# Four edits to a two-layer gated cross-attention kernel: output banks of the last FFN, lead-in of the second attention, start of the quantised down product, slot order of the first attention

## The reference, cut to what matters

```python
x = x + tanh(g_xattn[0]) * attention0(layernorm(x), ctx)   # 16 heads of 16, biases on q, k, v, out
x = x + tanh(g_ffn[0])   * ffn0(layernorm(x))              # 256 -> 768 gate and up, 4-bit block-quantised
                                                           # weights, activations rounded to 16-bit codes
x = x + tanh(g_xattn[1]) * attention1(layernorm(x), ctx)   # 8 heads of 64
x = x + tanh(g_ffn[1])   * ffn1(layernorm(x))              # 256 -> 1024, butterfly, exact gelu, butterfly,
                                                           # 1024 -> 256
# ffn0: every act_qdq needs the largest |value| of its whole tensor before one code can be made
#   o = act_qdq(act_qdq(gate * sig) * up);  return o @ lpbq_dequant(w_down).T
# ffn1, seen as the kernel computes it: the two butterflies are linear, so they are folded into the weights
#   y = gelu(x @ W1 + b1) @ W2 + b2
```

## Time and profile before

| what | value |
|---|---|
| median of 3 runs | 1124.44 us |
| profiled execution: its own time | 1123.65 us |
| its span | 1121.8 us |
| TensorE busy | 971.8 us (87%) |
| VectorE busy | 789.1 us (70%) |
| ScalarE busy | 620.1 us (55%) |
| mean granted TensorE clock | 0.934 |

### The profile page before, as it was taken

One profiled execution on the slowest core, in us unless ns is written; L12 is line 12 of the kernel. 1 busy time (PEld: TensorE's weight loads), 2 busy tenths in 40 slices (PEclk: granted clock), 3 DMA queues, 4 the chain that ended last, 5 costly groups with the idle time before them and its releaser, 6 DMA issues. The chain is left out here.

```text
span 1121.8 us, 20570 instructions
## 1 busy us (share of the span) xinstructions
PE 971.8 (87%) x6833; PEld 862.0 (77%) x6833; DVE 789.1 (70%) x1588; ACT 620.1 (55%) x1088; POOL 231.4 (21%) x424
## 2 busy tenths in 40 slices
PE   6489999998399997546699976999999989999998
PEld 5367788876378876445689965999999977888888
DVE  5358888865369888879678725677777858556662
ACT  4157766665367699779477435555656533222230
POOL 4223333311186000000022202111112113111210
PEclk9789999999689998867899986999999989999999
DMA  6745555560233077598333455755555410001001
GB/s 193 222 122 142 141 145 148 148 218 10 107 130 150 29 236 243 194 334 308 121 108 115 162 192 131 166 121 123 123 123 123 98 39 1 19 20 38 19 20 38
DMA packets 102807, 143.60 MB, mean 128 GB/s; under 512 B 42950, under 2 KB 76742, under 8 KB 100438
## 3 DMA queue, kind: packets, MB, share of 16 engines
q1 hardware_dynamic: 102438, 141.67, 43.7%
q0 software_dynamic: 304, 1.10, 0.3%
HBM read 76.30 MB, written 47.13 MB: 110 GB/s over the span
## 5 line engine op out<-in xcount | busy, mean ns | idle before, releaser
L41 PE MATMUL bank<-f_xt_hi,f_w_hi 128*128 128x512 f32 x320 | 130.1, 406 | 11.9 <-DMA f_xt_lo<-x_spill 8.7
L42 PE MATMUL bank<-f_xt_lo,f_w_hi 128*128 128x512 f32 x320 | 127.3, 398 | 0.0
L43 PE MATMUL bank<-f_xt_hi,f_w_lo 128*128 128x512 f32 x320 | 127.0, 397 | 0.0
L2635 ACT ACTIVATE f_h<-bank,f_b 128x512 f32<-128x512 f32 x64 | 43.4, 691 | 122.3 <-PE bank L43 74.5
L599 ACT ACTIVATE a_prob<-bank 77x512 f32<-77x512 f32 x128 | 72.7, 593 | 21.1 <-PE bank L763 20.9
L41 PEld LDWEIGHTS bank<-f_xt_hi,f_w_hi 128*128 128x128 f32 x320 | 61.8, 193 | 27.9 <-DMA f_xt_lo<-x_spill 10.8
L665 DVE TENSOR_REDUCE a_maxima<-bank 128x4 f32<-128x308 f32 x128 | 60.7, 474 | 31.8 <-PE bank L738 30.1
L41 PE MATMUL bank<-f_w_hi,f_h_hi 128*128 128x256 f32 x256 | 72.6, 284 | 8.1 <-DVE xres L2600 8.1
L43 PE MATMUL bank<-f_w_hi,f_h_lo 128*128 128x256 f32 x256 | 72.2, 282 | 0.0
L42 PE MATMUL bank<-f_w_lo,f_h_hi 128*128 128x256 f32 x256 | 72.2, 282 | 0.0
L43 PEld LDWEIGHTS bank<-f_xt_hi,f_w_lo 128*128 128x128 f32 x320 | 61.7, 193 | 13.4
(11 more groups left out here) (317 smaller groups left out, 3066.3 us busy)
## 6 DMA issues: line engine op xcount, KB each, us to landing
u_spill<-f_ubuf SPq DMA_DIRECT2D x48, 256.0 KB, 2.5
f_uback<-u_spill SPq DMA_DIRECT2D x24, 512.0 KB, 5.8
a_stack<-a_queries SPq DMA_DIRECT2D x16, 512.0 KB, 4.8
a_q_max<-a_q_hi SPq DMA_DIRECT2D x32, 256.0 KB, 4.8
a_kb<-a_key_spill SPq DMA_DIRECT2D x96, 77.0 KB, 2.5
f_mats<-in_low_steps SPq DMA_DIRECT2D x12, 512.0 KB, 6.8
xres<-in_x SPq DMA_DIRECT2D x16, 256.0 KB, 4.4
a_queries<-a_q_hi SPq DMA_DIRECT2D x16, 256.0 KB, 3.0
```

Source lines behind the costliest of these rows:

```text
L41: nc.tensor.matmul(out, w_hi, m_hi, start=start, stop=False)
L42: nc.tensor.matmul(out, w_hi, m_lo, start=False, stop=False)
L43: return nc.tensor.matmul(out, w_lo, m_hi, start=False, stop=stop)
L2635: act.activation(h[:, n % 2, :], hbank[n % 4][:, :], ACT.Gelu, bias=b1[:, n:n + 1]).then_inc(h_ready, 1)
```

## The change

1. Last FFN: four banks for the four y tiles, the two new ones being banks three and four of the h products. The waits follow: y tile n of a group waits for tile n of the group before; y tiles 2 and 3 also wait until the GELU has read the seventh and eighth h product of the next group out of those banks; the third and fourth h product wait for the adds of y tiles 2 and 3.
2. Quantised FFN, last block: `hi` moves up among the weight units on ScalarE, and `prod` on TensorE; the rounding of the first queries goes ahead of the last three value moves; both halves of the values are fetched after the last save instead of the first half after the sixth save.
3. Second attention: for the first batch ScalarE issues the four query transfers, and the two small ones for the gate and bias; SyncE's step is skipped; the second `pick` rounding goes behind the first queries' roundings; GpSimd clears `q_max` before `kz`.
4. First attention: other orders in PE_SLOT, ACT_SLOT and DVE_SLOT (the strings for the lead-in slots stay).

```diff
-        DVE_SLOT = "w0 mx0 norm mx1 ln mx2 w1 w2 w3 mx3 xs mx4 am w4 mx5 as mx6 w5 mx7 qs pu st1".split()
+        DVE_SLOT = "mx0 xs mx1 norm mx2 w0 w1 w2 mx3 ln mx4 w3 mx5 as mx6 am w4 mx7 qs pu st1 w5".split()
...
                 if what == "qm":
                     if isinstance(b, int) and b == 0:
-                        sp.wait_ge(mt_cleared, HPC)
+                        return
...
-                    if isinstance(b, int) and b == 0:
-                        sp.dma_start(gate_raw[:], gate).then_inc(small_in, 16)
-                        sp.dma_start(bo_raw[:], gbias).then_inc(small_in, 16)
...
-            pool.memset(kz[1][:].bitcast(F32), 0.0).then_inc(kb_cleared, 1)
             for a in range(HPC):
                 pool.memset(q_max[a][:].bitcast(F32), 0.0).then_inc(mt_cleared, 1)
+            pool.memset(kz[1][:].bitcast(F32), 0.0).then_inc(kb_cleared, 1)
...
+                    if isinstance(b, int) and b == 0 and n == 1:
+                        pick(1)
+                        act.wait_ge(q_rounded, NP)
+                        for q in (q_both, q_max):
+                            if q is q_max:
+                                act.wait_ge(mt_cleared, HPC)
+                            for a in range(HPC):
+                                act.dma_start(q[a][own[a], par, :, :].bitcast(F32),
+                                              q_hi[own[a], :, :].bitcast(F32)).then_inc(hi_in[par], 16)
...
-                    if i == NV // 2:
-                        fetch_values(0, i)
+                fetch_values(0, NV)
                 fetch_values(1, NV)
...
-                for n in range(4):
+                weights(0)
+                hi(0)
+                weights(1)
+                weights(2)
+                hi(1)
+                weights(3)
+                weights(4)
+                hi(2)
+                for n in range(5, 9):
                     weights(n)
-                hi(0)
-                weights(4)
-                hi(1)
-                weights(5)
-                weights(6)
-                hi(2)
-                weights(7)
-                weights(8)
                 hi(3)
...
-                for n in range(5):
+                for n in range(3):
                     weights(n)
                 prod(0)
-                for n in range(5, 7):
+                for n in range(3, 5):
                     weights(n)
                 prod(1)
-                for n in range(7, 9):
+                for n in range(5, 9):
                     weights(n)
...
-        ybank = [O0, O1]
+        ybank = [O0, O1, hbank[2], hbank[3]]
...
-                    if not (isinstance(g, int) and g == 0 and n < 2):
-                        pe.wait_ge(y_added, g * GTT + n - 1)
+                    if n >= 2:
+                        last_h = min(g + 2, G) if isinstance(g, int) else g + 2
+                        pe.wait_ge(h_ready, last_h * HT + n - 3)
+                    if n < 2 and not (isinstance(g, int) and g == 0) or isinstance(g, int) and g == G - 1:
+
+                        pe.wait_ge(y_added, g * GTT + n + 1 - GTT)
```

More of the change, by code:

```diff
@@ L406, in stacked_attention @@
         Q_MOVES, K_MOVES = 2, 6
-        PE_SLOT = "s0 s1 t3 mx0 s2 s3 mx1 xt p1 s4 mx2 s5 at0 mx3 p3 s6 mx4 s7 p5 mx5 q0 t0 mx6 t1 q1 mx7 pr0 pr1 mt t2 p7".split()
-        ACT_SLOT = "s0 s1 s2 s3 st2 s4 p1 xt s5 at0 p3 s6 xn q1 p5 s7 mt p7".split()
-        DVE_SLOT = "w0 mx0 norm mx1 ln mx2 w1 w2 w3 mx3 xs mx4 am w4 mx5 as mx6 w5 mx7 qs pu st1".split()
+        PE_SLOT = "s0 s1 xt mx0 s2 t3 s3 mx1 s4 q0 mx2 p1 s5 mx3 p3 s6 mx4 s7 at0 mx5 t0 q1 mx6 p5 t1 mx7 pr0 pr1 mt t2 p7".split()
+        ACT_SLOT = "s0 s1 xt s2 st2 s3 p1 s4 s5 p3 s6 at0 q1 s7 xn p5 mt p7".split()
+        DVE_SLOT = "mx0 xs mx1 norm mx2 w0 w1 w2 mx3 ln mx4 w3 mx5 as mx6 am w4 mx7 qs pu st1 w5".split()
         POOL_SLOT = "ln xn st1".split()
@@ L1060, in _, with pick @@
         def _(act):
+            def pick(n):
+                act.activation(kb[:, n, :, 1, :, :], late["pick_raw"][:, :, :, 0:S], ACT.Copy).then_inc(picked, 1)
             def step(what, b, par):
@@ L1063, in step @@
                     if isinstance(b, int) and b == 0:
+                        act.dma_start(gate_raw[:], gate).then_inc(small_in, 16)
+                        act.dma_start(bo_raw[:], gbias).then_inc(small_in, 16)
                         act.wait_ge(late["pick_in"], 16)
-                        for n in range(2):
-                            act.activation(kb[:, n, :, 1, :, :], late["pick_raw"][:, :, :, 0:S], ACT.Copy).then_inc(picked, 1)
+                        pick(0)
                         return
@@ L2301, in _ @@
                             round_key(n)
+                    if b == 16:
+                        act.wait_ge(first.xt_ready, 1)
+                        act.activation(xt_hi, T1[:, :].rearrange("p (c t) -> p c t", c=DC), ACT.Copy).then_inc(first.xt_rounded, 1)
                     for i in range(NV):
@@ L2322, in _ @@
                         last.then_inc(first.ln_xn, 1)
-                    if b == 16:
-                        act.wait_ge(first.xt_ready, 1)
-                        act.activation(xt_hi, T1[:, :].rearrange("p (c t) -> p c t", c=DC), ACT.Copy).then_inc(first.xt_rounded, 1)
                     i, half = (b - 4) // 3, (b - 4) % 3
@@ L2599, in step @@
                     x = xtile(g, n)
-                    dve.scalar_tensor_tensor(out=x, in0=ybank[n % 2][:, 0:D], scalar=tg[:, 0:1], in1=x,
+                    dve.scalar_tensor_tensor(out=x, in0=ybank[n][:, 0:D], scalar=tg[:, 0:1], in1=x,
                                              op0=ALU.mult, op1=ALU.add).then_inc(y_added, 1)
@@ L2655, in step @@
                         pe.wait_ge(xt_split, (g + 1) * DC)
-                    if not (isinstance(g, int) and g == 0 and n < 4):
+                    if n in (2, 3) and not (isinstance(g, int) and g < 2):
+                        pe.wait_ge(y_added, g * GTT + n - 3 - GTT)
+                    elif not (isinstance(g, int) and g == 0 and n < 4):
                         pe.wait_ge(h_ready, g * HT + n - 3)
@@ L2665, in step @@
                         pe.wait_ge(h_split, (g + 1) * HT)
-                    if not (isinstance(g, int) and g == 0 and n < 2):
-                        pe.wait_ge(y_added, g * GTT + n - 1)
+                    if n >= 2:
[3 more added lines that the diff above has]
+                        pe.wait_ge(y_added, g * GTT + n + 1 - GTT)
                     for m in range(HT):
-                        last = three_passes(nc, ybank[n % 2][:, 0:D], h_hi[:, par, m, n * P:(n + 1) * P],
+                        last = three_passes(nc, ybank[n][:, 0:D], h_hi[:, par, m, n * P:(n + 1) * P],
                                             h_lo[:, par, m, n * P:(n + 1) * P], w2_hi[:, m, :], w2_lo[:, m, :],
```

## The result

The kernel before took 1124.51 us in the median of 4 runs (1119.17 to 1129.31), the changed kernel 1110.58 us in 4 (1108.23 to 1113.65). The ratio is 0.9874, 95% interval 0.9828 to 0.992. Later, beside 11 runs of before, six more runs of the changed kernel gave 0.9898 (0.9851 to 0.9944). The profiled execution took 1113.65 us, with a span of 1111.9; that of before had a span of 1121.8. It is 9.9 us shorter.

The account below looks back on a forecast made before the run. The prediction took TensorE, busy 87% of the span, to set the pace, with time lost at its stops. Its terms, 9.6 + 0.8 + 6.8 - 1.0 = 16.2 us off 1123.65, gave 1107.5 us; range 1101 to 1113.5.

Parts of the forecast that it names:

- Last FFN: Last FFN: with four banks TensorE no longer stops six times for VectorE's adds; 9.6 us gained, low end 8.1.
- The lead-in: Second attention, opening to first scores: queries come earlier, but both value halves precede the keys; 1.0 us lost, bounds +1.6 and -4.6.
- the second rival: Second attention's lead-in: values, keys and queries share the DMA engines, first scores at +17.6 instead of +14.0; 1111 us, chance 0.14.
- the prediction's own sign: Forecast is wrong if the last FFN's groups keep 25 us, or the seam's stop only moves into the next block.
- what-is-late-next: Last FFN: GELUs end 1.5 us before y tiles 2 and 3 need them; adds have over 4 us of margin.
- the third rival: Last FFN: adds of y tiles 2 and 3 or the GELUs hold up TensorE for half the gain; 1112 us, chance 0.06.
- Down product's start: Quantised FFN's down product: starts 3.3 us earlier, but two units now follow; 0.8 us gained, bounds -2.8 and +3.3.
- Seam: Quantised FFN to second attention: first query matmuls start 5.5 us sooner and at full clock; 7.8 us gained.
- Slot orders: First attention: a 0.29 us hole goes every second slot, small waits are added; net 0.1 a slot, 1.0 us lost.
- the keys' loop: First attention: 7.2 us from last scores to `mx0`, while query and key transfers are issued and land; expected to stay.
- The first rival: First attention: the slot orders pay and slots take 13.17 us; 1102 us in all, chance 0.14.
- the fourth: First attention: ScalarE paces the slots, each losing about 1.5 us, 13 times; 1126 us, slower than before, chance 0.05.

Follow-up runs that it names:

- the banks and codes alone: Kernel before with only the last FFN's four banks and the codes' rounding moved up among the weight units; 1117.06 us, ratio 0.9918.
- the run with the slot orders alone: Kernel before with only the three new slot orders of the first attention; 1126.29 us, ratio 1.0009.
- the pair of the seam alone: Kernel before plus early rounding of x and both value fetches after the last save; with ScalarE's transfers 1127.06 us, with SyncE issuing 1125.53.
- the pair with the second half late: Changed kernel with the values' second half fetched behind the second batch's keys: 1105.73 and, again, 1104.6 us; with SyncE issuing queries, gate and bias 1109.35.
- the seam and lead-in kernel: Kernel before plus early rounding of x, both value fetches after the last save, and ScalarE issuing gate, bias and queries; 1127.06 us, ratio 0.9987.

## Why the prediction was right, and which term was not

It forecast 16.2 us off; the medians show 13.9 (1124.51 - 1110.58), the second measurement 10.5 (1124.24 - 1113.78). The terms as measured below give 9.4 + 2.1 + 1.5 - 0.8 = 12.2. The profiled pair differs by less, 9.9: the changed one had its long last slot (5.3 us against it), while the one before took 2.4 us more from its first scores to the last FFN.

The direction was earned, by the last FFN above all. That the time fell so near was in part luck. The lead-in was wrong by 5.4 us; the down product gave 1.3 more than forecast, and the first median lay 1.7 us below what the terms give. The first median, 1110.58, is where the second rival had put it (1111), not the forecast of 1107.5, and the second, 1113.78, lies just outside the range of 1101 to 1113.5. By the prediction's own sign, that the seam's stop only moves into the next block, its seam part failed: of 7.8 us won at the seam 6.4 were lost behind it.

- **Last FFN: 9.6 forecast, 9.4 measured** (9.1 with the banks and codes alone). The mechanism and its what-is-late-next held: neither the GELUs nor the adds stopped TensorE more than before, so the third rival (bank wait under another name) was wrong.
- **Down product's start: 0.8 forecast, 2.1 measured.** The start came 3.28 us sooner, as worked out (3.3). The units that now follow cost 2.75 (gaps behind the first two products 2.57 + 3.26, before 1.55 + 1.53), near the 2.5 said. What was left open was the clock: the first product took 4.42 us instead of 5.89, since the granted clock was 1.00 from 556 to 560, where before it was 0.78. The clock has a part in the 3.28 too. In before the weight units ran at 0.50 (545 to 547), and the product came 9.32 us after the transposes; in the run with the slot orders alone, with the same units in front at 1.00, it came after 7.64. With the new order it is 6.04 to 6.20 in all nine profiles, so the order itself is worth 1.6 to 3.3 us. Over nine profiles of the new order and five of the old, the whole stage takes 113.9 and 115.6 us in the mean, so 1.7 us is the better figure.
- **Seam: 7.8 forecast, 7.9 measured**: from the last down product to the last query product 665.63 - 662.80 = 2.83 us, before 670.13 - 659.43 = 10.70. 5.5 of it is the stop, the rest the clock at 1.00.
- **Lead-in: 1.0 lost forecast, 6.4 measured** (from the last query product to the first scores 21.37 us, before 15.01), or 5.6 counted from ScalarE's first copy, ahead of which two transfers now stand. This term was mis-sized, and its bound too near: +17.6 against +18.6 and, in the second profile of the changed kernel, +19.3. Seam and lead-in together gave 1.5 us instead of 6.8. The cause had been named, values ahead of keys, and the volume nearly so: 4.2 MB reckoned, 4.52 moved. The rate was not. I took 248 and 204 GB/s from stretches of before and chose "the value of the faster row", a stretch in which mostly values moved; the real one ran at 190. So the stretch took 23.8 us instead of 17.0. Of the 6.8 more, the rate makes 5.2 (4.2 MB at 190 instead of 248) and the 0.32 MB more 1.7. As the values were issued 5.2 us ahead of the opening and not 3.0, 14.0 + 6.8 - 2.2 = 18.6. The second rival (transfers collide), held at 0.14, is what happened, and it went 1.0 us beyond even its +17.6.
- **ScalarE as issuer.** Nothing gained in the changed kernel: 24.04 us to the first scores with, 23.96 without, in the pair of the seam alone. The Trainium skill (DMA: Bandwidth & Descriptors, "Rules for kernel authors") says that more issuing engines save only issue time. These runs agree, and so does the pair with the second half late: what ScalarE saved there was issue time on SyncE, 3.5 us at the fetch of the values. But that time stood in front of what the next batch needed, and so it came back as 3.9 us at the third batch.
- **Slot orders: 1.0 lost forecast, 0.8 found, in another place.** The forecast made it of 0.1 us in ten slots. The slots don't show it: from the first to the fifteenth copy of the maxima the eight profiles with the new order took 189.3 to 193.4 us (mean 191.5), the six with the old 188.9 to 192.1 (mean 190.7), and the means differ by less than the profiles of one order do. In both, the keys' loop, named in the prediction, holds TensorE up: it waited for keys 4.1 to 7.2 us between 50 and 240 us in the old order, 4.2 to 7.8 in the new. The 0.8 stands behind the last slot, the same in all profiles (27.15 against 26.32), where TensorE now waits twice for exponentials, 0.6 us together, as the row at 274.99 shows; no profile of the old order has that wait. The first rival (orders pay) and the fourth (ScalarE paces) are wrong: no slots of 13.2 us throughout, and none of 15 but the last.
- **The last slot** of the changed kernel's profile, 5.3 us too long, is not the order's doing alone: with the old order it took 13.17 to 17.08 us in six profiles, with the new 13.49 to 21.28 in eight. Whether the new order makes the long ones likelier stays open; six and eight are too few.

## What to carry to other kernels

When a stop goes and a stage opens sooner, list everything that is issued between the old opening and the first consumer, with its bytes, and divide by the rate of a stretch with the same kind of transfers, not by the best one. Then ask of each large transfer when it is first read: here half of the values was needed only from the ninth batch on, and moving its issue behind the second batch's keys was worth 5 to 9 us by the medians, more than the seam repair and the new lead-in had brought together (1.5 us by the profile, none by the medians). Moving small transfers to another queue paid here only after that, and a large transfer moved back must not land in front of the next batch's small ones.

## What the runs showed of the hardware

One issue of a key transfer of 77 KB took 7.36 us (6.78 in the seam and lead-in kernel, 5.41 in the second profile of the changed one), where most took 0.65: a queue can hold its issuing engine. All three had two fetches of 1.28 MB outstanding on that queue and ScalarE's transfers beside it. With the same two fetches and no transfers of ScalarE the longest such issue took 1.96 us; why is not shown. A bias of 128 KB, issued on ScalarE's queue ahead of the queries, landed after 10.7 us in the changed kernel and after 4.3 with the second half late. And the clock's answer to a short wait varied: after 2.08 us without work it fell to 0.50 for some 10 us in the changed kernel, while after 2.17 us at the same place in the kernel run again with the second half late it read 1.00 before and after:

```profile
258.83 0.46 PE L738 MATMUL bank<-a_kb,a_stack 96*128 96x156 f32 x2 [2.17 <-DMA a_kb<-a_keys]
254.00:258.00 4.00, 2.65 (x25) 1.79 (x23) 1.88 (x6) 1.83 (x4) 1.04 (x3) 1.00 0.89 196
258.00:262.00 4.00, 3.11 (x28) 2.53 (x28) 1.76 (x6) 2.06 (x4) 0.49 (x3) 1.00 0.02 5
```

Kernels with the same, old slot order took 13.17 to 17.08 us for the last slot, so a single profile of such a stretch proves little.
